# A fully unrolled slot schedule put into a loop of fourteen passes on five engines

## The reference

```
W = weights[condition]                       # (64, 128, 128), one of 16 matrices per batch
x = x + einsum('bct,bcd->bdt', x, W)         # layer 0: mixes the channels
K[h, l] = 2 * Re( sum_n Ct[h,n] * exp(dtA[h,n] * l) )      # 64 modes for each channel
y = causal convolution of x[b, h, :] with K[h, :]          # by FFT of length 4096
y = (y + x * D[h]) * (t < length[b])
x = x + y                                    # layer 1
```

## Time and profile before

| | |
|---|---|
| median of three runs | 1104.54 us |
| profiled execution | 1108.28 us |
| its span, first to last instruction | 1106.4 us |
| outside the span | 1.9 us |
| mean granted TensorE clock | 0.978 of full speed |
| PE busy | 1008.3 us, 91% |
| DVE, ACT, POOL busy | 624.6, 547.2, 453.2 us |
| stage 1 | up to about 333 us |
| stage 2 | from about 333 us to the end |

### The profile page before, as it was taken

One profiled execution on the slowest core, in us unless ns is written; L12 is line 12 of the kernel. 1 busy time (PEld: TensorE's weight loads), 2 busy tenths in 40 slices (PEclk: granted clock), 3 DMA queues, 4 the chain that ended last, 5 costly groups with the idle time before them and its releaser, 6 DMA issues.

```text
span 1106.4 us, 24650 instructions
## 1 busy us (share of the span) xinstructions
PE 1008.3 (91%) x9478; PEld 745.8 (67%) x9478; DVE 624.6 (56%) x1518; ACT 547.2 (49%) x1163; POOL 453.2 (41%) x542
## 2 busy tenths in 40 slices
PE   6987789777756999999999999999999999999997
PEld 2332344223214888888888888888888888888886
DVE  6989910000002666666666666666666666666664
ACT  2633344343433555555555555555555555555553
POOL 3211043000203545556556556455455565564520
PEclk9999999899985999999999999999999999999999
DMA  9999999999997698999999999899999999999984
GB/s 336 415 425 422 424 422 418 384 424 424 424 401 216 163 225 227 226 226 228 225 221 226 230 223 227 226 228 215 232 228 221 230 225 231 222 225 229 222 202 115
DMA packets 220227, 305.17 MB, mean 276 GB/s; under 512 B 79874, under 2 KB 178562, under 8 KB 211922
## 3 DMA queue, kind: packets, MB, share of 16 engines
q1 hardware_dynamic: 219426, 302.37, 93.5%
q10 hardware_dynamic: 528, 1.05, 0.3%
q0 software_dynamic: 160, 0.20, 0.1%
HBM read 152.37 MB, written 134.41 MB: 259 GB/s over the span
## 4 chain that ended last, share of the span: by engine, by line
PE 70%; DMA 24%; ACT 4%; issue 1%; SPq 0%; DVE 0%; ACTq 0%
DMA u_scratch<-stage 23%; PE bank L461 23%; PE bank L467 15%; PE bank L426 13%; PE bank L412 10%; PE bank L438 6%; ACT stage L533 3%; PE bank L400 2%; DMA x_f<-in_x 1%; DMA u_row<-u_scratch 0%; DVE st_sb L798 0%; ACT st_sb L554 0%; ACT L505 0%; ACT waves L508 0%; ACT waves L505 0%
## 5 line engine op out<-in xcount | busy, mean ns | idle before, releaser
L461 PE MATMUL bank<-toep,u_t 128*128 128x256 f16 (+1 forms) x3072 | 394.5, 247 | 0.0
L467 PE MATMUL bank<-g_sb,st_sb 128*128 128x256 f16 x1536 | 306.3, 273 | 0.0
L400 PE MATMUL bank<-x_f,w_buf 128*128 128x512 f32 x512 | 242.1, 621 | 63.3 <-ACT stage L533 51.3
L793 DVE SCALAR_TENSOR_TENSOR u_t<-bank,u_t 128x512 f16<-128x512 f32 x256 | 176.4, 689 | 218.5 <-ACT u_t L546 218.5
L461 PEld LDWEIGHTS bank<-toep,u_t 128*128 128x128 f16 x3072 | 280.3, 98 | 24.9
L412 PE MATMUL bank<-ident,u_row 128*128 128x128 f32 x1024 | 280.1, 278 | 16.6 <-DMA u_row<-u_scratch 14.8
L554 ACT ACTIVATE st_sb<-bank 128x128 f16<-128x128 f32 x448 | 123.8, 276 | 296.3 <-PE bank L438 203.7
L798 DVE TENSOR_TENSOR st_sb<-bank,st_sb 128x128 f16<-128x128 f32 x448 | 130.7, 292 | 192.7 <-ACT st_sb L554 190.4
L400 PEld LDWEIGHTS bank<-x_f,w_buf 128*128 128x128 f32 x512 | 96.5, 197 | 204.5 <-issue 112.6
L806 DVE COPY_PREDICATED o_sb<-mask,u_row 128x512 f32<-128x512 uint8 x256 | 213.1, 832 | 16.8 <-issue 16.7
L533 ACT ACTIVATE stage<-bank 128x1024 f32<-128x1024 f32 x128 | 123.9, 1021 | 174.1 <-DMA u_scratch<-stage 157.0
(11 more groups left out here) (118 smaller groups left out, 475.9 us busy)
## 6 DMA issues: line engine op xcount, KB each, us to landing
x_f<-in_x SPq DMA_DIRECT2D x64, 1024.0 KB, 19.6
u_scratch<-stage SPq DMA_DIRECT2D x64, 1024.0 KB, 17.7
u_row<-u_scratch SPq DMA_DIRECT2D x128, 512.0 KB, 5.4
out<-o_sb SPq DMA_DIRECT2D x256, 256.0 KB, 3.8
toep<-k_scratch SPq DMA_DIRECT2D x64, 256.0 KB, 5.4
gt_sb<-g_sb SPq DMA_TRANSPOSE x128, 4.6
nat<-in_L_cond_C SPq DMA_DIRECT2D x2, 64.0 KB, 4.9
k_scratch<-k_body POOLq DMA_DIRECT2D x4, 32.0 KB, 7.1
```

The costliest lines, as they stand in the source:

```text
L400: last = pe.matmul(bank[:, 4 * (n % 2) + k, :], w_buf[n % XS][:, :], x_f[n % XS][:, k * 512:(k + 1) * 512], start=True, stop=True)
L461: pe.matmul(bank[:, y, col + tb * P:col + Q], lhs, t[:, h, b, 0:Q - tb * P], start=first, stop=False, skip_group_check=True)
L467: last = pe.matmul(bank[:, y, col:col + Q], st[:, h, a, gr * ROWS:(gr + 1) * ROWS], g[:, h, b, :], start=False, stop=(m == 2), skip_group_ ...
L793: dve.scalar_tensor_tensor(out=t[:, q // 2, q % 2, 1, :], in0=bank[:, 4 + q, :], scalar=US, in1=t[:, q // 2, q % 2, 0, :], op0=MUL, op1=SU ...
```

## The change

`slots` now makes three pieces: slots 0 to 2 as before, then a loop that each engine runs for itself, with a counter `i` in a register, `i = 0 .. 13`, and a body of four slots, and then slots 59 to 65 as before. The same 66 slots are run in the same order.

```diff
         def slots(eng, body):
-            for c in range(PAIRS + 2):
+            for c in range(PEELED):
+                body(0, c)
+            with eng.Fori(0, LOOPS) as i:
+                for c in range(PEELED, PEELED + UN):
+                    body(i, c)
+            for c in range(UN * LOOPS + PEELED, PAIRS + 2):
                 body(0, c)
```

## The result

The changed kernel takes 1113.68 us (median of four runs, 1111.53 to 1114.65) against 1104.61 (1102.98 to 1108.28) before: ratio 1.0075, 95% interval 1.0045 to 1.0104. It is 9 us slower. Forecast were 42 us and 1146; 1113.68 lies inside the stated range, but the predicted slowdown is four and a half times too large, and the case that came true is one that the prediction gave as a rival, with a time that was too good.

What follows compares the result with a forecast made beforehand. PE, with no idle time in stage 2, was taken as the bound; 35 us for refetching after branches plus 7 us for register steps made 42, added to 1104.5 for 1146 us. The stated range was 1103 to 1168 us.

Steps and rivals of the forecast that it cites:

- (a): PE's loop end: target instructions fetched again at each of 13 jumps back, PE standing 2.7 us each, 35 us.
- the body stays resident: Rival at the loop's end: PE keeps its body, branch hidden under work in hand, 1103 us, no change; chance 0.22.
- called itself wrong under 1.5: Sign in stage 2: the forecast is wrong if PE's idle time per pass is under 1.5 us.
- The price of a fetch: At each jump back: one fetch takes 3.0 us, ends 2.0 and 5.4, including 0.92 for the packet.
- the clock stays at 1.00: Sign between PE's idle times in stage 2: the granted clock stays full, 2.4 GHz.
- work in hand: Array work PE still has where the loop closes: 0.17 to 0.41 us, taken as 0.3 and subtracted from the fetch.
- The third rival: PE's body resident, but register arithmetic exposed in more places than a slot's start: 1120 us, 1144 at full; chance 0.17.
- small gaps in every slot: Sign of the third rival: small gaps on PE ahead of L461, L412 and L438 in every slot.
- Step (b): PE's register arithmetic at slot starts: two uncovered steps of 0.06 us in each of 56 slots, 7 us; ends 0 and 39.
- Step (c): Register arithmetic and branches on the other engines: nothing, their own fetches falling while PE stands for its own.
- What is given back: Stage 2: less fetching gives nothing; if uneven slots came from fetching, at most 3 us over 56 slots.

Runs made afterwards that it cites:

- experiments 5 to 7: Changed kernel with eight slots in the loop body: 1151.11 us; then also matmuls left out on PE, bodies 1749 and 1621 instructions: 73 and 18 packets on queue 8.
- experiment 2: Changed kernel with PE run straight and only ACT, DVE, POOL and SP in loops: 1104.53 us, ratio 1.0000 against the kernel before.
- experiments 3 and 9: Changed kernel with PE's loop closed elsewhere: behind the inputs-to-state product, 1107.08 us; just ahead of the wait for a slot's last state, 1107.30 us.
- Experiment 4: Changed kernel with the loop of 14 passes written out as 14 loops of one pass on all engines: 1108.77 us, ratio 1.0033.

## Why the prediction was wrong

**The step that failed is (a), the branch back.** It said that the target "must be fetched again while PE stands", for 2.7 us a pass, 35 us in all. Nothing is fetched again with a body of 1198 instructions (20 packets; experiments 5 to 7 put the limit between 1621 and 1749, for bodies placed as these are), and PE's idle time at a jump is 0.43 us, where the prediction called itself wrong under 1.5. The rival "the body stays resident" was right on this, and I gave it 0.22. What I had for the forecast was a rule, and a trace of a straight program that could not tell: "nothing in the trace shows a piece used twice" was no argument against. The Trainium skill's sentence on a two-page window ("Runtime: NRT & Kernel Launch", instruction fetch mechanics) is contradicted for PE by these runs, where a body of 6.3 pieces is still there. Its 128 KB on TensorE ("Advanced Engine Details and Errata", ISA Cache) are eight pieces of 16 KB, and the runs agree with that if one piece is being refilled.

**The price of a fetch was too low as well.** Where it does happen it costs 7.2 us, not 2.7: the branch takes 4.0 to 5.7 us, near the upper end of my bounds (5.4) and not near the 3.0 that I took. The packet itself, 1.4 us on the mean against my 0.92, is the smaller part; 2.2 us before it and 1.4 behind it are the rest. And I left out that PE, once it has stood that long, goes on at half clock, another 2 us. I had written that the clock stays at 1.00.

**The rival's own time, 1103, failed at "a few tenths of a us, under the work in hand".** The size was near: 0.40 us for the branch with its arithmetic, and three or four steps of up to 0.1 more than before. What failed is the cover. That the array has at most 0.17 to 0.41 us of work in hand was read rightly from the earlier trace rows, and so was the reason, the wait for DVE's state just ahead. But I took this work as free to hide something new. The straight program already uses it for its own two waits, and its next load of weights comes just as the array runs out (719.228 against 719.255). So next to nothing of the branch and the steps is hidden, and 0.74 us are paid. Moving the loop's end (experiments 3 and 9) gave back most of it.

**The third rival** (1120 us, 0.17) is the nearest by its number, and it was right that the steps are exposed although the body is resident. But it put them into every slot, and its sign, small gaps in every slot, is not there: the price stands at the jumps alone.

**Step (b), the register arithmetic, was about right in sum and wrong in place.** Forecast 7 us, at every slot's start. Of the 0.74 us at a jump back, some 0.34 are register steps (0.74 - 0.40), which is 4.4 us in 13; at the other 43 slot starts they cost at most 0.02 (11.68 against 11.66). 0.06 us for one step was too low: it is about 0.1 from start to start, of which 0.03 to 0.06 is its record.

**Step (c) was right**: nothing for the other engines (experiment 2), though for (c) I had named PE's own standing as the cover, and none was needed. **What is given back was right** as a bound: "at most 3 us" were 2.2; the sum had put it at nothing.

## What to carry to other kernels

Read from the profile how much work the bound engine has in hand at the place where its loop will close; behind a wait on another engine that is a few tenths of a us, and the branch and the register steps for the new pass come on top of each other there. Do not take that work as free: look at what the program already does in that time. Close the loop where the engine's program is about to wait, or behind long instructions. Count the instructions of the body on each engine before anything else: kept, a jump back cost 0.2 to 0.7 us here, by its place; not kept, it cost 7.2 on PE, with the half clock behind it, so that unrolling a loop twice as far made this kernel 3% slower than the loop of four.

## What the hardware showed that I had not expected

The straight program's slots are not all equal, and the long ones follow the pieces in which its program is fetched. Its slots of 11.79 us come in runs. Numbering PE's instructions in the order of the trace, all gaps between its matmuls that are over 0.06 us too long from 400 to 1080 us (16 of them: 15 of 0.08 to 0.17 us and one of 0.58) lie within 90 instructions behind a multiple of 256 (plus 193), that is, I take it, behind the end of a piece; in the loop of four the boundaries fall at the same places in each pass, none of them close ahead of a slot's start, and these gaps are gone. Being there is not enough: of the 21 slots of that stretch that start within 90 instructions behind such a place, 10 have no gap. The trace of experiment 2, which has the same program on PE, repeats 15 of the 16, all but the one of 0.58. Experiment 4 moves the boundaries a little, because its loops add instructions: away from the loops' ends it has 13 such gaps, partly in other slots, and they too lie 0 to 80 instructions behind a boundary. So the place is borne out; that it is the fetching, and not something else at the end of a piece, is not shown.

The same compare and branch has a record of 208 ns on PE but of 45 on ACT and POOL and 54 to 56 on SP and DVE. The records mislead, though: from the start of the branch to the next instruction of the engine it is 0.27 us on PE, 0.27 on ACT, 0.29 on DVE, 0.30 on SP and 0.24 on POOL. The branch costs about the same on each; it is paid on PE because PE has no time to spare there.
